# A decoder layer on one core: twelve of sixteen batches sent to their experts by indirect stores, four kept dense

## What is computed

```python
shared_out = (silu(x @ shared_gate_w) * (x @ shared_up_w)) @ shared_down_w
probs = softmax(x @ gate_w)                       # 64 experts
topk_w, topk_idx = top_k(probs, 8)                # 8 of them per token
topk_w = topk_w / sum(topk_w)
combine = zeros((T, 64)).at[arange(T)[:, None], topk_idx].add(topk_w)
for e in range(64):                               # each expert: 256 -> 64 -> 256
    acc += combine[:, e] * ((silu(x @ gate_e) * (x @ up_e)) @ down_e)
out = acc + sigmoid(x @ shared_expert_gate_w) * shared_out
```

## Time and profile before

| What | Value |
|---|---|
| Time, median of 3 runs | 1114.79 us |
| Lowest and highest of the 3 | 1114.3 and 1116.24 us |
| Profiled execution, first to last instruction (span) | 1116.6 us |
| Profiled execution's own device time | not listed apart from its span; the highest run shown, 1116.24 us, is 0.4 us below the span |
| PE, DVE, ACT, POOL busy | 1070.9, 640.7, 545.0, 638.0 us |
| Attention and projections | 0 to 407 us |
| Cross-attention with the router of 8 batches | 407 to 542 us |
| MoE, 66 slots | 542 to 1116 us |

### The profile page before, as it was taken

One profiled execution on the slowest core, in us unless ns is written; L12 is line 12 of the kernel. 1 busy time (PEld: TensorE's weight loads), 2 busy tenths in 40 slices (PEclk: granted clock), 3 DMA queues, 4 the chain that ended last, 5 costly groups with the idle time before them and its releaser, 6 DMA issues.

```text
span 1116.6 us, 22413 instructions
## 1 busy us (share of the span) xinstructions
PE 1070.9 (96%) x7512; PEld 875.3 (78%) x7512; DVE 640.7 (57%) x1454; ACT 545.0 (49%) x1142; POOL 638.0 (57%) x772
## 2 busy tenths in 40 slices
PE   5988999999999989999899999999999999999997
PEld 4767777777777767766688888888888888888887
DVE  6756877778877788897767642323333323233233
ACT  2426767676676657676433453333343333333333
POOL 3675766757588332223455556566566566666664
PEclk9978999999999999999999999999999999999999
DMA  5201111111112066661333343443444443343342
GB/s 138 68 1 26 29 32 39 36 40 36 40 27 49 2 152 153 154 159 52 91 99 100 91 113 104 118 113 99 112 118 137 111 119 99 104 124 101 99 122 72
DMA packets 75232, 97.11 MB, mean 87 GB/s; under 512 B 20540, under 2 KB 55996, under 8 KB 75148
## 3 DMA queue, kind: packets, MB, share of 16 engines
q1 hardware_dynamic: 75148, 96.05, 33.0%
HBM read 82.73 MB, written 13.12 MB: 86 GB/s over the span
## 4 chain that ended last, share of the span: by engine, by line
PE 79%; DVE 9%; issue 4%; POOL 3%; ACT 2%; DMA 2%; SPq 1%; DVEq 0%; ACTq 0%; POOLq 0%
PE bank L1899 30%; PE bank L1915 16%; PE bank L682 3%; PE bank L684 3%; PE bank L634 2%; PE bank L711 2%; PE bank L341 2%; PE bank L623 2%; PE bank L1445 2%; PE bank L1470 2%; PE bank L715 1%; PE bank L1368 1%; PE bank L612 1%; PE bank L740 1%; PE bank L658 1%
## 5 line engine op out<-in xcount | busy, mean ns | idle before, releaser
L2135 POOL TENSOR_TENSOR hidden<-act_u,comb 128x512 f32<-128x512 f32 x131 | 208.8, 1594 | 227.2 <-DVE act_u L2068 148.4
L2068 DVE TENSOR_TENSOR act_u<-act_g,bank 128x512 f32<-128x512 f32 x128 | 88.0, 688 | 334.2 <-ACT act_g L2024 165.1
L2024 ACT ACTIVATE act_g<-bank 128x512 f32<-128x512 f32 x132 | 79.1, 599 | 337.1 <-PE bank L1899 337.0
L1899 PE MATMUL bank<-x_hi,up_hi 128*128 128x512 f32 x512 | 203.8, 398 | 2.8 <-POOL up_lo L2120 2.7
L1899 PE MATMUL bank<-x_hi,up_lo 128*128 128x512 f32 x512 | 203.0, 397 | 0.0
L1899 PE MATMUL bank<-x_lo,up_hi 128*128 128x512 f32 x512 | 202.3, 395 | 0.0
L872 ACT ACTIVATE probs<-bank 128x512 f32<-128x512 f32 x192 | 113.9, 604 | 85.5 <-PE bank L684 48.3
L1915 PE MATMUL bank<-down_hi,h_hi 128*128 128x256 f32 x528 | 151.1, 286 | 2.3 <-DVE h_lo L2073 1.8
L1915 PE MATMUL bank<-down_hi,h_lo 128*128 128x256 f32 x528 | 149.9, 284 | 0.0
L1915 PE MATMUL bank<-down_lo,h_hi 128*128 128x256 f32 x528 | 149.8, 284 | 0.0
L1899 PEld LDWEIGHTS bank<-x_hi,up_lo 128*128 128x128 f32 x512 | 96.5, 188 | 22.5
(11 more groups left out here) (271 smaller groups left out, 2196.9 us busy)
## 6 DMA issues: line engine op xcount, KB each, us to landing
comb<-combine_scratch SPq DMA_DIRECT2D x130, 256.0 KB, 3.8
up_in<-in_w_up SPq DMA_DIRECT2D x66, 256.0 KB, 3.6
down_in<-in_w_down SPq DMA_DIRECT2D x66, 128.0 KB, 3.7
keys_x<-key_rows_x SPq DMA_DIRECT2D x32, 192.0 KB, 3.4
ctx_in<-in_ctx SPq DMA_DIRECT2D x32, 128.0 KB, 2.1
key_rows_x<-ctx_hi SPq DMA_DIRECT2D x256, 16.0 KB, 1.5
query_x<-xq_rows_hi SPq DMA_DIRECT2D x64, 64.0 KB, 3.2
key_rows_x<-ctx_lo SPq DMA_DIRECT2D x128, 16.0 KB, 1.5
```

What stands on the lines that cost most here:

```text
L1899: last = nc.tensor.matmul((GATE, UP)[s][h][:], wp[p][:, c, s, :], xp[:, c, t:t + 512], start=k == 0, stop=k == 5)
L2024: nc.scalar.activation(act_g[h][:], GATE[h][:], ACT.Silu).then_inc(S(f"gated{h}"), 1)
L2068: ins = nc.vector.tensor_tensor(act_u[h][:], act_g[h][:], UP[h][:], ALU.mult)
L2135: nc.gpsimd.tensor_tensor(hidden[h][:], act_u[h][:], comb[p][:, 512 * h:512 * h + 512], ALU.mult)\
```

## The change

Twelve batches (`NS = 12`) leave the dense MoE. For each of them the router writes 128 normalised token rows eight times into a DRAM tensor `xs`, once per chosen expert, at a slot that is the token's rank in that expert's list. POOL does this with 96 indirect DMAs of 128 rows of 1 KB. Every expert has room for 1536 rows; its first 128 make a tile that is always computed, and 96 further tiles go to the experts that have more rows (their places come from a table that is computed on the chip and read into registers of PE and SP). So there are 160 tiles of 128 rows. For each of them, in plain float32 and without the split, PE turns the rows, multiplies by gate and up, turns the hidden rows and multiplies by down, and SP stores the result to `ys`. Then POOL fetches for each token its eight results with 96 indirect DMAs, and DVE adds them to X with the token's weights. Meanwhile the last four batches go through the dense MoE of 32 pairs in one half of 512 tokens, with POOL's two multiplies moved to DVE. The shared expert is taken out of the dense loop and computed for all tokens between cross-attention and tiles; the two shared projections ride on the router's matmul, which grows from 65 to 193 columns. All expert weights (up 8.4 MB, down 4.2 MB) are loaded once and stay in SBUF.

Also moved: the router of r = 0 to 8 lies between the cross-attention's steps from step 36 on (`START`), no longer in batches 14 and 15 alone; the query normalisation (L1411) goes from POOL to ACT; `xs` is filled with zeros by sixteen 512 KB DMAs during attention; from step 48 on the row maxima use two PSUM banks, not three; many semaphores are used a second time (`AGAIN`).

```diff
-PASS = 1024
-ROUTED = 4
+NS = 12
+CAP = NS * T
+EXTRA = CAP * K_TOP // 128
+TILES = E + EXTRA
+DENSE_T = (B - NS) * T
+R_ALL = E + 1 + 2 * I
+XROW_RING = 5
+GOT_RING = 24
+START = (36, 46, 57, 67, 76, 86, 96, 106, 116)
...
         def cross_loads(sp):
...
+                if b >= B:
+                    for j in range(10 * (b - B), 10 * (b - B + 1), 5):
+                        load_up(sp, j, j + 5)
...
         def cross_pool(pool):
-            for b in range(4, B):
-                cross_query(pool, b)
-                cross_query_low(pool, b - 1)
+            for r in range(NS):
+                pool.wait_ge(S("slots_ready"), ended("slots_ready") + r + 1)
+                for k in range(8):
+                    if (r, k) in between:
+                        cross_query_low(pool, between[r, k])
+                    nc.gpsimd.indirect_dma_start(
+                        out=xs, out_offset=bass.IndirectOffsetOnAxis(ap=slot_idx[:, r, k:k + 1], axis=0),
+                        in_=xrow[r % XROW_RING][:], in_offset=None).then_inc(S(f"sent{r % XROW_RING}"), 16)
...
+        def route_rank(pe, r):
+            nc.tensor.matmul(out, ones_b[0:1, :], first_slot[0:1, :], start=True, stop=False)
+            for q in range(r):
+                nc.tensor.matmul(out, ones_b[:], chosen[:, q, :], start=False, stop=False)
+            nc.tensor.matmul(out, up_to[:], chosen[:, r, :], start=False, stop=True).then_inc(S("rank_done"), 1)
...
+        def sparse_loads(sp):
+            def load(p):
+                if p >= BUFS:
+                    sp.wait_ge(S("tile_turned"), ended("tile_turned") + 2 * (p - BUFS) + 2)
+                if 2 * p < E:
+                    sp.dma_start(buf[:].bitcast(F32), rows[0:128, 2 * p:2 * p + 2, :]).then_inc(S(f"ld_tile{q}"), 16)
+                    return
+                for a in range(2):
+                    sp.dma_start(buf[:, a, :].bitcast(F32), xs[ds(regs[2 * p + a - E], 128), :])\
+                        .then_inc(S(f"ld_tile{q}"), 16)
...
+        def sparse_tensor(pe):
+            pe.wait_ge(S("shared_added"), ended("shared_added") + B // 2)
+            pe.wait_ge(S("ld_up_res"), ended("ld_up_res") + 16 * 7)
+            pe.wait_ge(S("ld_down_res"), ended("ld_down_res") + 16 * 8)
+            for j in range(TILES + 3):
+                values(j)
+                if j < TILES:
+                    turn(j)
+                if 0 <= j - 1 < TILES:
+                    up(j - 1)
+                if 0 <= j - 2 < TILES:
+                    turn_hidden(j - 2)
+                if 0 <= j - 3:
+                    down(j - 3)
...
+        def combine_pool(pool):
+            for n in range(len(y_tile)):
+                pool.wait_ge(S(f"y_out{n}"), 16 * len(range(n, TILES // 2, len(y_tile))))
+            for g in range(8 * NS):
+                if g >= GOT_RING:
+                    pool.wait_ge(S("combined"), ended("combined") + g - GOT_RING + 1)
+                nc.gpsimd.indirect_dma_start(
+                    out=got[g % GOT_RING][:], out_offset=None, in_=ys,
+                    in_offset=bass.IndirectOffsetOnAxis(ap=slot_idx[:, r, k:k + 1], axis=0))\
+                    .then_inc(S(f"got{g % GOT_RING // 4}"), 16)
...
+        def dense_vector(dve):
+            for n in range(E // 2):
+                if n + 1 < E // 2:
+                    up_low(n + 1)
+                if n:
+                    hidden_low(n - 1)
+                weighed(n)
+                down_low(n)
+                for k in range(3 if n >= 2 else 0):
+                    combine(dve, g)
+                    g += 1
```

1417 lines of the change are left out of this document (886 added, 531 removed).

## The result

The changed kernel takes 1040.24 us (median of 4 runs, 1037.51 to 1041.79) beside 1115.43 for the one before: 0.9328 of it, 95% interval 0.9312 to 0.9343. The forecast was 945 us with a range of 885 to 1060; the sign and the range held, the size did not: 6.7% faster instead of 15%. The profiled execution has a span of 1038.3 us.

What follows compares the result with a forecast made beforehand. PE alone was taken to bound the MoE. Cross-attention ending at 552, then 40 to the first tile, 206 for tiles and 148 for the dense part gave 946.5, less 1.8 is 945 us; range 885 to 1060.

Steps and rivals of the forecast that it cites:

- The tiles, forecast 206: 160 tiles: 64 first ones at 1.05 us, 96 extra at 1.40, plus 5 for DVE's reductions; bounds 149 and 320.
- Cross-attention, forecast +10: Cross-attention: routing nine batches between its steps adds 10 us, bounds 0 and +30, so the stage ends at 552.
- DVE six operations at 0.21 [...]; both have more room than PE: Cross-attention, per routed batch: DVE's six small operations and ACT's four copies fit, as both have more room than PE.
- Between the stages, forecast 40: Cross-attention to first tile: 32 us of new serial work, 40 with some 30 handovers; bounds 30 and 60.
- the clock stays down in the tiles: Tiles, rival: clock falls between the stages and stays low, a tile takes 2.1 us, total 1058; chance 0.13.
- The dense part, forecast 148: Dense MoE: 32 pairs at 4.35 us set by DVE, 139, plus start, drain, last additions and stores: 148 us.
- three fetches 3.7 against 4.35: both are covered: Dense part: three fetches per pair at 1.22 us of POOL each take 3.7, hidden under a 4.35 us pair.
- The place of the break: Indirect stores and fetches: cover ends for both near 1.45 us per transfer; 1.22 was taken.
- the rival of a hindered POOL: Stores and fetches, rival: POOL kept from writing transfers beside DVE; slower than before from 2.34 us each; chance 0.04.
- The 3.1 us of the other rule: Indirect transfers: skill's rule that a GpSimd-issued DMA takes about 3100 ns beside a DVE copy; would give 1262 us.
- PE's pace (888): Tiles, rival: they run at PE's pace, 160 x 0.90 + 5 = 149 us instead of 206; chance 0.15.
- Indirect transfers as the bound (1013): Stores and fetches, rival: at 1.80 us each, stores end 34 us late and pairs add 34 more; chance 0.17.

Runs made afterwards that it cites:

- experiment 1: Changed kernel with the tiles' down product filled up to 128 rows by zeros: 1079.7 us, in a series where every changed kernel took 1072 to 1123; tile 1.21 us.
- experiment 6: Changed kernel with DVE's statistics operations spread three or five at a time over the next cross-attention steps: 1031.5 us beside 1041.7 unspread (1121.5, 1122.5 in slow series).
- experiment 4: Changed kernel without the 96 indirect stores, extra tiles reading the first ones' rows: 1033.5 us both times, 7.4 and 8.2 below the unmodified changed kernel.
- two controls: The changed kernel run again unmodified beside the variants; over three series it took 1040.9, 1041.7 and 1041.7 us.
- experiment 3: Changed kernel with the tiles' down product at 128 rows and 44 filler products on PE between cross-attention and tiles: 985.8 us, 0.8854 of the kernel before.

## Why the prediction was right and wrong

**Direction, and what bounds the kernel: right.** PE at full clock is the bound of tiles and of most of the dense part, and the gain comes from its work.

**The tiles, forecast 206, measured 252: the largest error, and two steps of mine failed in it.** The first is "four float32 products of 256 columns take 1.03 [...] so one takes 0.22" and what rests on it, 0.85 us of PE for a tile. The four entries are two products; the tile's PE work is 1.21 us, 160 times some 0.35 us more, 56 us in all. The second is that I priced PE's instructions one by one and put nothing on the change from 128 to 64 rows of weights: 0.34 us a tile, 54 us, shown by experiment 1. Against these stand terms that I had and that are nothing: handovers (0.2 a tile, 32 us), the register loads with addresses (0.35 for each extra tile, 34) and DVE's reductions (5). So 71 us charged for nothing hid most of 110 that were missing; that the tiles were off by only 46 us, and that the range held, is luck; had those terms been real, the time would have been 1111 us. By PE alone, correctly counted, the sum would have been 1.21 x 160 = 194 us; the 64 rows bring it to 248, and most of the rest to 252 is the half clock of the first 6 us. The rule cited for register loads (the Trainium skill, "DMA: Bandwidth & Descriptors", "Latency and other measured facts", 600 ns) would have given 29 us; the trace has 0.33 us each on PE's sequencer, hidden here, and 10 us for all of them once the tile is 1.21.

**Cross-attention, forecast +10, measured +38.** The step that failed is "DVE six operations at 0.21 [...]; both have more room than PE". DVE has room on the mean, but the statistics come in pieces of 3.2 us, and PE waits 2.6 to 4.0 behind four of the five: 11.4 us, by experiment 6. The indirect stores, forecast at nothing, are 3 to 5 (experiment 4). The router's products, at up to 0.2 each in the forecast, are 0.32 by the corrected price of a float32 product (193 of 256 columns of 0.43 us), 2 us over nine batches. The shift rows, forecast at 3, show 1.7 (2.6 and 3.1 in two controls), and these are part of what the stores cost. Of the 28 us, some 10 to 13 are assigned by no experiment. The profile shows some of it: PE waits 3.9 us for ACT's copies of the rows to be routed (L1898 and L1912), and its busy time grew by 12.5 us, where 7 were forecast.

**Between the stages, forecast 40, measured 49.** The serial work was right in kind. The rival "the clock stays down in the tiles" looked for the price in the wrong place: the clock was back 6 to 11 us behind the start of the first tile, but the products of the shared expert ahead of the tiles ran at 0.50, and this is most of the 9 us (experiment 3: the shared expert's 16 down products and the turns among them take 8.3 us where they took 16.1).

**The dense part, forecast 148, measured 157.** "DVE waiting for fetched rows [...] says that they cost more than 1.45" came true: 1.51 on the mean. The steps that failed are "three fetches 3.7 against 4.35: both are covered", about 4 us in the pairs, and the 8 us for drain, additions and stores, where 13 lie behind the last pair. The place of the break was right; the value (1.22 taken) was a sum of two things, 0.95 + 0.30 when POOL is left alone, which is 1.25, and up to 1.5 more beside DVE's operations on two SBUF tiles. The forecast had the rival of a hindered POOL, but took both kinds of transfer to be hit alike. The stores were not: their maximum is 1.22 us, beside DVE's maxima, which read PSUM. On the page "SBUF — State Buffer" the Trainium skill says, under "Who interferes with whom", that an operation with two SBUF inputs contends only with a GpSimd instruction that reads SBUF, and it takes descriptor writing to be free of it, as inferred. Here the fetches are held up beside just such subtractions, 2.42 us instead of 0.95, so this trace speaks against that inference, or a fetch also reads SBUF, its addresses for one. The measurement decides either way. The 3.1 us of the other rule were not reached: no more than two such operations of 0.69 us stand together here, and a fetch is through 0.82 us after the second.

**The rivals.** PE's pace (888) named the right mechanism of the tiles with the wrong price. Indirect transfers as the bound (1013) held for the later dense pairs only.

## What to carry to other kernels

Before a duration is divided by a count from the profile, the entries must be matched with the instructions of the code: a float32 product has two entries, and the price taken from the quotient was half of what it should be. Where small products of different row counts alternate, filling the smaller one up with zeros may be faster than the smaller one: here 1.21 instead of 1.55 us for the round. An engine with room on the mean still stops others when its work comes in one piece, so what matters is the longest piece between two results that someone waits for, and this holds for POOL's issues beside DVE's row as well: another operation between two subtractions was worth 12 us here.

## What was not expected of the hardware

- Weights of 64 rows between weights of 128: 0.20 us more at the down product and 0.15 at the turns behind it in a tile; products of 64 rows one behind the other cost nothing more.
- Register loads on PE: 0.33 us each on its sequencer, no effect on a tile of 1.55 us, 0.08 us per tile on one of 1.21.
- An indirect transfer of 128 rows of 1 KB takes POOL 0.96 us and 0.30 to the next; beside subtractions of two SBUF tiles on DVE it took up to 2.43, and every one above 1.3 us in these traces ended 0.82 us after an operation of DVE on two SBUF tiles of 128x512.
- Two series in which kernels with indirect transfers took far longer (77 to 80 and 90 to 91 us more for the two that were also measured outside them), with engines standing still while POOL issued, and in which the kernel before, without such transfers, did not change.
